# Window attention beside a mixture of experts: two key halves in one product, and the softmax passage one step later

## The chip, the cores and the metric

The kernel runs on one core of one Trainium2 chip. The metric is device microseconds of one execution. The kernel before takes 686.98 us, the median of 3 runs (686.58 to 687.01). All times are in us unless ns is said.

## The reference

```python
xn = layernorm(x)                                    # x: 32 sequences of 256 tokens, 128 channels
# attention branch
h = relu(xn @ nm_w1 + nm_b1);  m = h @ nm_w2 + nm_b2
q, k, v = m @ q_w + q_b, m @ k_w + k_b, m @ v_w + v_b
scores = (q . k in a window of 32 tokens to either side) / sqrt(128)
a = softmax(scores) @ v (over the window)
# expert branch: 16 experts, the 8 best per token, and a shared one
s = sigmoid(xn @ gate_w.T);  chosen = top8(s + expert_bias);  c = 2.826 * s / sum(s of chosen)
y = sum over experts e of c[e] * (silu(xn @ w_gate[e].T) * (xn @ w_up[e].T)) @ w_down[e].T
y = y + the same with the shared weights, without c
out = x + a + y
```

All of it is float32. Every big operand is split into a high part that the product engine takes as it is and a low rest, and a product of two such operands is three products: high by high, high by low, low by high.

## The kernel before, in words

The 8192 tokens go through in 16 groups of 512 (two sequences of 256, each in two tiles of 128 queries). A group has 17 steps: step 0 is the shared expert, steps 1 to 16 the routed ones. Each engine has a program written by hand (`slot(g, par, s)`), walked through group by group and step by step; the attention and the routing of the same and of the next group are hung into its steps (`when(g, s, fresh)` gives the step, with another one for group 0; `more` and `last` leave out what the last group doesn't need). Nothing else orders the work: every engine runs its list in order and waits on semaphores.

For step k of a group I write:

- gate(k) and up(k): three products of 512 columns each on PE into `ps_g` and `ps_u` (two banks each, used in turn), lines 466 and 476. gate(k) waits until silu(k-2) is done, up(k) until h_lo(k-2) is done.
- silu(k): ACT, line 717, from `ps_g`. silu_c(k): POOL, line 1262, times the routing weight.
- h(k): DVE, line 1134, silu_c times `ps_u` in place. h_hi(k): ACT, line 725, the high part. h_lo(k): DVE, line 1140, the rest.
- down(k): three products of 512 on PE into `ps_y`, line 486.

In its step s PE issues gate(s+1), down(s-3) and up(s), ACT h_hi(s-1) and silu(s+1), DVE h(s-1) and h_lo(s-1), POOL silu_c(s+1). Between these stand, for the group's attention:

- PE: `scores(seq)`, line 430, one bank per sequence, both tiles of queries in it, three products of 160 columns for each tile (step 3 for sequence 0, step 5 for sequence 1); `turn_probs(seq)`, line 437, three transposes of 128 columns (end of step 7, and step 9); `attend`, line 447, products of 256 and 160 columns (steps 13 and 14); `value_proj`, line 456, in step 0 of the next group; `hid_proj` of the next group, three products of 512, at the end of step 7 behind the transposes; the gate product of the router (`gate`, line 419) in step 4.
- POOL: `mask_terms(seq)`, line 1246: the window mask plus a term for each key, two operations for each sequence.
- DVE: `row_max(seq)`, line 1025: score plus mask and the row's maximum in one operation for each tile; `normalise_probs`, lines 1033 and 1037; `gate_sum` (step 5), lines 866 and 870, four transposes and a sum of the router's product; `route_scores` (step 7), lines 877 to 881; then the choice of 8 and the weights in steps 8 to 11, for the next group.
- ACT: `gate_exp` (router, line 674) and `prob_exp(0)` (line 706) in step 5, `prob_exp(1)` in step 6 behind h_hi(5), the two table loads around them (silu and the exponential are in different tables), `prob_hi` in steps 7 and 9.

So ACT's list between silu(6) and silu(7) is: table load, the router's exponential, two exponentials, h_hi(5), two exponentials, table load. I call this the passage.

## Time and profile before

| what | value |
|---|---|
| median of 3 runs | 686.98 us |
| profiled execution | 687.21 us, span 685.4 us |
| PE busy | 676.9 us, 99% of the span |
| PE weight loads | 553.8 us, 81% |
| DVE busy | 597.6 us, 87% |
| ACT busy | 437.2 us, 64% |
| POOL busy | 443.0 us, 65% |
| granted clock of PE | 9 or more tenths in all 40 slices |
| chain that ended last | PE 90%, DVE 4%, DMA 3%, ACT 1%, issue 1% |

The chain is followed back from the last instruction: at each step to what released it, or to the instruction before it on its engine. Busy time of PE says little by itself, because matmuls are pipelined and their ends are modelled; the starts of successive products in the timeline say how long each really takes.

### The profile page before, as it was taken

How to read it: one execution, taken by the hardware profiler on the slowest of the kernel's cores; microseconds unless marked ns; L12 is line 12 of the kernel's file. 1: busy time of each engine (PE TensorE's matmuls, PEld its weight loads, DVE VectorE, ACT ScalarE, POOL GpSimd, SP SyncE). 2: the span in 40 equal slices, each digit the busy share in tenths (PEclk: the TensorE clock that was granted, in tenths of full speed). 3: DMA queues.
4: the chain of work that ended last, by engine and by line, in shares of the span. 5: the costliest groups of instructions: out<-in, count | busy, mean ns of one | idle time of the engine just before them, and what ended most of it. 6: DMA issues, size and time to landing. Idle time of an engine off the chain costs nothing.

```text
span 685.4 us, 10455 instructions
## 1 busy us (share of the span) xinstructions
PE 676.9 (99%) x3172; PEld 553.8 (81%) x3172; DVE 597.6 (87%) x1640; ACT 437.2 (64%) x874; POOL 443.0 (65%) x400
## 2 busy tenths in 40 slices
PE   7999999999999999999999999999999999999997
PEld 6877788888888888888888888888888888888885
DVE  7998989888889898889888898898889888898775
ACT  5775656657675575666657665575756757666573
POOL 4785666666667756766666667766667567666553
PEclk9999999999999999999999999999999999999999
DMA  8607255252623617155261633617145161631500
GB/s 266 236 9 272 61 186 185 93 232 73 233 113 124 235 46 277 62 173 198 65 260 51 252 116 104 254 45 278 63 163 208 49 262 47 220 121 63 231 0 16
DMA packets 38040, 101.80 MB, mean 149 GB/s; under 512 B 8672, under 2 KB 18144, under 8 KB 29920
## 3 DMA queue, kind: packets, MB, share of 16 engines
q1 hardware_dynamic: 37984, 101.14, 41.1%
q8 instruction: 25, 0.41, 0.2%
q14 instruction: 31, 0.25, 0.1%
HBM read 92.42 MB, written 8.70 MB: 148 GB/s over the span
## 4 chain that ended last, share of the span: by engine, by line
PE 90%; DVE 4%; DMA 3%; ACT 1%; issue 1%; SPq 1%; POOL 0%; DVEq 0%; ACTq 0%
PE ps_y L486 26%; PE ps_u L476 26%; PE ps_g L466 25%; PE bank L408 3%; PE bank L447 3%; PE bank L430 3%; PE bank L437 1%; PE ps_y L456 1%; DMA exp_raw<-wexp 1%; DMA h_dram<-exp_raw 1%; DVE ps_u L1134 1%; PE bank L419 1%; DVE h_lo L1140 1%; DMA exp_raw<-h_dram 0%; DVE prob_n L1037 0%
## 5 line engine op out<-in xcount | busy, mean ns | idle before, releaser
L1262 POOL TENSOR_TENSOR silu_c<-silu,comb_b 128x512 f32<-128x512 f32 x252 | 325.3, 1294 | 220.5 <-ACT silu L717 219.6
L725 ACT ACTIVATE h_hi<-ps_u 128x512 fp32r<-128x512 f32 x272 | 162.9, 599 | 232.9 <-DVE ps_u L1134 232.8
L1140 DVE TENSOR_TENSOR h_lo<-ps_u,h_hi 128x512 fp32r<-128x512 f32 x272 | 186.0, 684 | 37.3 <-ACT h_hi L725 30.4
L1134 DVE TENSOR_TENSOR ps_u<-silu_c,ps_u 128x512 f32<-128x512 f32 x256 | 177.1, 692 | 28.5 <-PE ps_u L476 24.2
L717 ACT ACTIVATE silu<-ps_g 128x512 f32<-128x512 f32 x272 | 162.0, 596 | 0.2
L476 PE MATMUL ps_u<-xn_hi,exp_w_hi 128*128 128x512 f32 x272 | 111.2, 409 | 0.7 <-DVE h_lo L1140 0.6
L486 PE MATMUL ps_y<-h_hi,exp_w_hi 128*128 128x512 f32 x272 | 109.4, 402 | 0.9 <-DVE h_lo L1140 0.4
L466 PE MATMUL ps_g<-xn_hi,exp_w_hi 128*128 128x512 f32 x272 | 108.1, 397 | 1.3 <-ACT silu L717 1.3
L486 PE MATMUL ps_y<-h_lo,exp_w_hi 128*128 128x512 f32 x272 | 107.7, 396 | 0.0
L476 PE MATMUL ps_u<-xn_hi,exp_w_lo 128*128 128x512 f32 x272 | 107.6, 396 | 0.0
L486 PE MATMUL ps_y<-h_hi,exp_w_lo 128*128 128x512 f32 x272 | 107.3, 394 | 0.0
L466 PE MATMUL ps_g<-xn_hi,exp_w_lo 128*128 128x512 f32 x272 | 106.9, 393 | 0.0
L476 PE MATMUL ps_u<-xn_lo,exp_w_hi 128*128 128x512 f32 x272 | 106.7, 392 | 0.0
L466 PE MATMUL ps_g<-xn_lo,exp_w_hi 128*128 128x512 f32 x272 | 105.8, 389 | 0.0
L476 PEld LDWEIGHTS ps_u<-xn_hi,exp_w_hi 128*128 128x128 f32 x272 | 51.2, 188 | 14.0 <-DVE h_lo L1140 3.2
L466 PEld LDWEIGHTS ps_g<-xn_hi,exp_w_hi 128*128 128x128 f32 x272 | 51.0, 188 | 13.9 <-issue 2.0
L486 PEld LDWEIGHTS ps_y<-h_hi,exp_w_lo 128*128 128x128 f32 x272 | 51.3, 189 | 12.2
L476 PEld LDWEIGHTS ps_u<-xn_hi,exp_w_lo 128*128 128x128 f32 x272 | 51.2, 188 | 12.2
L466 PEld LDWEIGHTS ps_g<-xn_lo,exp_w_hi 128*128 128x128 f32 x272 | 51.3, 188 | 12.1
L466 PEld LDWEIGHTS ps_g<-xn_hi,exp_w_lo 128*128 128x128 f32 x272 | 51.0, 188 | 12.3
L486 PEld LDWEIGHTS ps_y<-h_hi,exp_w_hi 128*128 128x128 f32 x272 | 51.2, 188 | 11.2 <-DVE h_lo L1140 0.8
L486 PEld LDWEIGHTS ps_y<-h_lo,exp_w_hi 128*128 128x128 f32 x272 | 51.3, 189 | 9.9
(156 smaller groups left out, 989.2 us busy)
## 6 DMA issues: line engine op xcount, KB each, us to landing
comb_b<-c_dram SPq DMA_DIRECT2D x63, 1024.0 KB, 7.2
mom_b<-st_dram SPq DMA_DIRECT2D x13, 512.0 KB, 3.7
xres<-x_t SPq DMA_DIRECT2D x16, 256.0 KB, 2.6
out_t<-xres SPq DMA_DIRECT2D x16, 256.0 KB, 2.0
xin<-x SPq DMA_DIRECT2D x15, 256.0 KB, 3.2
h_dram<-exp_raw SPq DMA_DIRECT2D x60, 64.0 KB
exp_raw<-h_dram SPq DMA_DIRECT2D x15, 256.0 KB, 3.1
xn<-x_t SPq DMA_DIRECT2D x13, 256.0 KB, 3.3
```

Of the source, the lines that this page charges most:

```text
L408: done = mm(dst[:], att_w[a][:, w, :], parts[b][:], start=n == 0, stop=n == 2)
L419: done = mm(bank[0][:], gate_w[:].rearrange("p q c -> p (q c)"), xn_t[par][n][:], start=n == 0, stop=n == 1)
L430: done = mm(dst[:, t * SEQ:t * SEQ + WIN], q_t[a][:, q0:q0 + P], hid_t[b][:, k0:k0 + WIN], start=n == 0, stop=n == 2)
L447: done = mm(bank[2][:, col:col + wide], hid_n[a][:, seq * 2 + kb, :], p_t[b][:, seq, kb, 0:wide], start=kb == 0 and n == 0, stop=kb == 1 a ...
L466: done = mm(ps_g[i][:], exp_w[a][:, s, 0:P], xn_t[par][b][:], start=n == 0, stop=n == 2)
L476: done = mm(ps_u[i][:], exp_w[a][:, s, P:2 * P], xn_t[par][b][:], start=n == 0, stop=n == 2)
L486: done = mm(ps_y[:], exp_w[a][:, s, 2 * P:3 * P], h_t[i][b][:], start=s == 0 and n == 0, stop=s == STEPS - 1 and n == 2, skip_group_check= ...
L717: A(silu[i][:], ps_g[i][:], ACT.Silu).then_inc(s_silu, 1)
L725: A(h_t[hbuf(par, s)][0][:], ps_u[(par + s) % 2][:], ACT.Copy).then_inc(s_h_hi, 1)
L1134: V.tensor_tensor(ps_u[i][:], src[:], ps_u[i][:], ALU.mult).then_inc(s_h, 1)
L1140: V.tensor_tensor(t[1][:], ps_u[(par + s) % 2][:], t[0][:].bitcast(F32), ALU.subtract)\
L1262: G.tensor_tensor(silu_c[i][:], silu[i][:], comb_b[:, s1 - 1, :], ALU.mult).then_inc(s_silu_c, 1)
```

## The change

All of it applies from group 2 on (`wide(g)`), groups 0 and 1 stay as they were except for the places of some steps.

- High and low part of the keys (`hid_t`) now lie in one tensor `hid_hl`. For each tile of queries, one product of 320 columns takes the high part of the queries against both halves of the keys, and one of 160 the low part of the queries against the high half, added to the front half of the result. Each tile of queries has its own bank (`window_bank`), so both sequences use the same two banks one after the other.
- The rear half (queries by low keys) is read by ACT (`low_scores`), which adds the key's term and writes `low_k`; POOL adds the mask in one operation for each sequence; `row_max` adds the front half and writes its result to `prob` in SBUF, where the exponentials and the normalising now read and write.
- `scores(0)` moves from step 3 to 2, `scores(1)` stays in 5 and now waits for the row maximum of sequence 0. `mask_terms(1)` moves on POOL from step 3 to 5. `row_max(1)` moves from 6 to 7, the exponentials from 5 and 6 to 6 and 7 (the router's with them), `normalise_probs(0)` from 6 to 7, `turn_probs` from 7 and 9 to 8 and 10 (the first now also waits for the second row maximum), `prob_hi` from 7 and 9 to 8 and 10, `prob_lo(1)` from 10 to 11. `hid_proj` stays at the end of step 7.
- `route_scores` stays in step 7 of DVE but goes from ahead of h_lo(6) to behind it.

```diff
-            def scores(seq):
+            def scores(g, seq):
+                if wide(g):
+                    for t in range(2):
+                        q0 = seq * SEQ + t * P
+                        k = slice(seq * SEQ + t * (P - HALF), seq * SEQ + t * (P - HALF) + WIN)
+                        dst = window_bank[t]
+                        mm(dst[:, 0:2 * WIN].rearrange("p (h c) -> p h c", h=2), q_t[0][:, q0:q0 + P],
+                           hid_hl[:, :, k], start=True, stop=False, skip_group_check=True)
+                        done = mm(dst[:, 0:WIN], q_t[1][:, q0:q0 + P], hid_hl[:, 0, k], start=False, stop=True,
+                                  skip_group_check=True)
+                    done.then_inc(S[f"sc{seq}"], 1)
+                    return
...
-                if s == when(g, 3, 5):
+                if s == when(g, 2 if wide(g) else 3, 5):
...
                 if s == when(g, 5, 7):
-                    scores(1)
+                    if wide(g):
+
+                        pe.wait_ge(S["nmax0"], g + 1)
+                    scores(g, 1)
...
-                if s == when(g, 9, 12):
+                if s == when(g, 10, 12):
                     pe.wait_ge(S["pn1"], g + 1)
                     turn_probs(1)
...
-                if s == when(g, 7, 10):
+                if s == when(g, 7, 10) and not last(g):
+                    hid_proj(g + 1, 1 - par)
+                if s == when(g, 8, 10):
                     pe.wait_ge(S["pn0"], g + 1)
+                    if wide(g):
+
+                        pe.wait_ge(S["nmax1"], g + 1)
                     turn_probs(0)
-                    if not last(g):
-                        hid_proj(g + 1, 1 - par)
...
+            def low_scores(g, seq):
+
+                act.wait_ge(S[f"sc{seq}"], g + 1)
+                act.wait_ge(S["key_term"], 2 * g + seq + 1)
+                for t in range(2):
+                    n = 2 * seq + t
+                    done = A(low_k[:, n, :], window_bank[t][:, WIN:2 * WIN], ACT.Identity, bias=key_term[:, n:n + 1])
+                done.then_inc(S[f"low{seq}"], 1)
...
-                if s == when(g, 5, 8):
+                if wide(g) and s == 2:
+                    low_scores(g, 0)
+                if wide(g) and s == 5:
+                    low_scores(g, 1)
+                if s == when(g, 6, 8):
                     if more:
                         gate_exp(g + 1)
                     prob_exp(g, 0)
...
-                if s == when(g, 6, 9):
+                if s == when(g, 7, 9):
                     prob_exp(g, 1)
...
-                if s == when(g, 6, 9):
+                if s == when(g, 7, 9):
                     normalise_probs(g, 0)
-                if s == 7 and more and not first(g):
-                    route_scores(g + 1)
...
-                if s == when(g, 6, 9):
+                if s == when(g, 7, 9):
                     row_max(g, 1)
...
-                if first(g) and s == 9:
-                    route_scores(1)
+                if s == when(g, 7, 9) and not last(g):
+                    route_scores(g + 1)
...
+                if wide(g):
+                    n = slice(2 * seq, 2 * seq + 2)
+                    pool.wait_ge(S[f"low{seq}"], g + 1 - (TURNED - 1))
+                    G.tensor_tensor(mask_k[:, n, :], mask[:], low_k[:, n, :], ALU.add).then_inc(S["mask_k"], 1)
+                    return
```

How the instructions now follow one another, at three places. On PE, the second block of scores of a group (step 5), with the gate products ahead of it and the down products behind; `q_hi`, `q_lo` are the queries, `hid_hi`, `hid_lo`, `hid_hl` the keys. Before:

```order
L466 MATMUL ps_g<-xn_hi,exp_w_lo 128x512
L430 MATMUL bank<-hid_hi,q_hi 128x160
L430 MATMUL bank<-hid_lo,q_hi 128x160
L430 MATMUL bank<-hid_hi,q_lo 128x160
L430 MATMUL bank<-hid_hi,q_hi 128x160
L430 MATMUL bank<-hid_lo,q_hi 128x160
L430 MATMUL bank<-hid_hi,q_lo 128x160
L486 MATMUL ps_y<-h_hi,exp_w_hi 128x512
```

Now:

```order
L492 MATMUL ps_g<-xn_hi,exp_w_lo 128x512
L445 MATMUL bank<-hid_hl,q_hi 128x320
L447 MATMUL bank<-hid_hl,q_lo 128x160
L445 MATMUL bank<-hid_hl,q_hi 128x320
L447 MATMUL bank<-hid_hl,q_lo 128x160
L512 MATMUL ps_y<-h_hi,exp_w_hi 128x512
```

Six products of 160 columns have become two of 320 and two of 160, each with its own weight load.

On ACT, the passage with its exponentials, from h_hi(4) on, in a group from 2 on; `bank` and `prob` are the scores, `low_k` the new rear half. Before:

```order
L725 ACTIVATE h_hi<-ps_u 128x512
L717 ACTIVATE silu<-ps_g 128x512
L674 ACT_TABLE_LOAD
L674 ACTIVATE gate_e<-gate_s 128x64
L706 ACTIVATE bank,row_sum<-bank,neg_max 128x160 x2
L725 ACTIVATE h_hi<-ps_u 128x512
L706 ACTIVATE bank,row_sum<-bank,neg_max 128x160 x2
L717 ACT_TABLE_LOAD
L717 ACTIVATE silu<-ps_g 128x512
```

Now:

```order
L768 ACTIVATE h_hi<-ps_u 128x512
L760 ACTIVATE silu<-ps_g 128x512
L742 ACTIVATE low_k<-bank,key_term 128x160 x2
L768 ACTIVATE h_hi<-ps_u 128x512
L760 ACTIVATE silu<-ps_g 128x512
L709 ACT_TABLE_LOAD
L709 ACTIVATE gate_e<-gate_s 128x64
L749 ACTIVATE prob,row_sum<-prob,neg_max 128x160 x2
L768 ACTIVATE h_hi<-ps_u 128x512
L749 ACTIVATE prob,row_sum<-prob,neg_max 128x160 x2
L760 ACT_TABLE_LOAD
L760 ACTIVATE silu<-ps_g 128x512
```

The passage began behind silu(6) and ended with silu(7); it now begins behind silu(7) and ends with silu(8), and two copies of scores stand where it was.

On DVE, from the router's sum in step 5 on; `ps_u` is h(k), the lines with ISA are the row maximum. Before:

```order
L870 TENSOR_REDUCE gate_s<-gate_h 128x64
L1140 TENSOR_TENSOR h_lo<-ps_u,h_hi 128x512
L1025 ISA bank,neg_max<-bank,mask_k 128x160
L1025 ISA neg_max 128x1
L1025 ISA bank,neg_max<-bank,mask_k 128x160
L1025 ISA neg_max 128x1
L1134 TENSOR_TENSOR ps_u<-silu_c,ps_u 128x512
L1033 RECIPROCAL row_inv<-row_sum 128x2
L1037 TENSOR_SCALAR prob_n<-bank,row_inv 128x160 x2
L1140 TENSOR_TENSOR h_lo<-ps_u,h_hi 128x512
L1134 TENSOR_TENSOR ps_u<-silu_c,ps_u 128x512
L877 TENSOR_SCALAR gate<-gate_e 128x64
```

Now:

```order
L1184 TENSOR_TENSOR h_lo<-ps_u,h_hi 128x512
L1071 ISA prob,neg_max<-bank,mask_k 128x160
L1071 ISA neg_max 128x1
L1071 ISA prob,neg_max<-bank,mask_k 128x160
L1071 ISA neg_max 128x1
L1178 TENSOR_TENSOR ps_u<-silu_c,ps_u 128x512
L1079 RECIPROCAL row_inv<-row_sum 128x2
L1083 TENSOR_SCALAR prob_n<-prob,row_inv 128x160 x2
L1184 TENSOR_TENSOR h_lo<-ps_u,h_hi 128x512
L924 TENSOR_SCALAR gate<-gate_e 128x64
L926 RECIPROCAL score<-gate 128x64
L928 TENSOR_TENSOR select<-score,ebias 128x64
```

Ahead of the second piece stand, now, the sum, h_lo(4) and h(5) alone: its first row is h_lo(5), and the row maximum of sequence 1 follows that instead of h_lo(4). The normalising goes with it, and the routing's scores have come behind h_lo(6).

## Rows read from the trace of the kernel before

**Rows 1.** Timeline of PE: start, duration, engine, line, operation; last value product, groups 7 and 8.
```profile
310.32 0.39 PE L456 MATMUL ps_y<-z_hi,att_w_lo 128*128 128x512 f32 x1
...
351.66 0.39 PE L456 MATMUL ps_y<-z_hi,att_w_lo 128*128 128x512 f32 x1
```

**Rows 2.** Timeline of PE: first block of scores in group 7, and products behind it.
```profile
316.11 0.24 PE L430 MATMUL bank<-hid_hi,q_hi 128*128 128x160 f32 x1
316.19 0.27 PE L430 MATMUL bank<-hid_lo,q_hi 128*128 128x160 f32 x1
...
317.02 0.39 PE L486 MATMUL ps_y<-h_lo,exp_w_hi 128*128 128x512 f32 x1
317.25 0.40 PE L486 MATMUL ps_y<-h_hi,exp_w_lo 128*128 128x512 f32 x1
```

**Rows 3.** Timeline of PE: the product of 256 columns in attend, group 7.
```profile
340.81 0.28 PE L447 MATMUL bank<-p_hi,hid_n_hi 128*128 128x256 f32 x1
340.93 0.23 PE L447 MATMUL bank<-p_lo,hid_n_hi 128*128 128x160 f32 x1
```

**Rows 4.** Timeline of PE: first products of gate(9) and gate(10), group 7.
```profile
328.68 0.40 PE L466 MATMUL ps_g<-xn_hi,exp_w_hi 128*128 128x512 f32 x1
...
330.76 0.40 PE L466 MATMUL ps_g<-xn_hi,exp_w_hi 128*128 128x512 f32 x1
```

**Rows 5.** Timeline of ACT: h_hi(4), silu(6), end of the first two exponentials, silu(7).
```profile
321.65 0.60 ACT L725 ACTIVATE h_hi<-ps_u 128x512 fp32r<-128x512 f32 x1 [1.38 <-DVE ps_u L1134]
322.15 0.59 ACT L717 ACTIVATE silu<-ps_g 128x512 f32<-128x512 f32 x1
...
324.86 0.20 ACT L706 ACTIVATION_READ_ACCUMULATOR bank<-bank,neg_max 128x1 f32 x1
...
327.73 0.60 ACT L717 ACTIVATE silu<-ps_g 128x512 f32<-128x512 f32 x1
```

**Rows 6.** Timeline of DVE: h(4), h_lo(4), h(5), h_lo(5), h(6), routing, h(7), h_lo(7).
```profile
320.92 0.70 DVE L1134 TENSOR_TENSOR ps_u<-silu_c,ps_u 128x512 f32<-128x512 f32 x1 [0.41 <-PE ps_u L476]
...
323.17 0.69 DVE L1140 TENSOR_TENSOR h_lo<-ps_u,h_hi 128x512 fp32r<-128x512 f32 x1
...
324.30 0.73 DVE L1134 TENSOR_TENSOR ps_u<-silu_c,ps_u 128x512 f32<-128x512 f32 x1
...
325.88 0.68 DVE L1140 TENSOR_TENSOR h_lo<-ps_u,h_hi 128x512 fp32r<-128x512 f32 x1
326.48 0.69 DVE L1134 TENSOR_TENSOR ps_u<-silu_c,ps_u 128x512 f32<-128x512 f32 x1
327.08 0.19 DVE L877 TENSOR_SCALAR gate<-gate_e 128x64 f32<-128x64 f32 x1
...
327.89 0.23 DVE L881 TENSOR_TENSOR select<-score,ebias 128x64 f32<-128x64 f32 x1
...
329.81 0.70 DVE L1134 TENSOR_TENSOR ps_u<-silu_c,ps_u 128x512 f32<-128x512 f32 x1 [0.27 <-POOL silu_c L1262]
...
331.51 0.68 DVE L1140 TENSOR_TENSOR h_lo<-ps_u,h_hi 128x512 fp32r<-128x512 f32 x1
```

**Rows 7.** Timeline of ACT and PE, last group: silu(7), second product of gate(9).
```profile
657.78 0.60 ACT L717 ACTIVATE silu<-ps_g 128x512 f32<-128x512 f32 x1
...
658.76 0.40 PE L466 MATMUL ps_g<-xn_lo,exp_w_hi 128*128 128x512 f32 x1
```

**Rows 8.** Groups by line and shape, whole span: count, busy us and mean ns.
```profile
L706 ACT ACTIVATE bank<-bank,neg_max 128x160 f32<-128x160 f32 x64 | 23.1, 360 | 0.0
...
L685 ACT ACTIVATE q_hi<-bank,vecs 128x512 fp32r<-128x512 f32 x16 | 11.2, 703 | 0.0
...
L670 ACT ACTIVATE xn_hi<-xn 128x512 fp32r<-128x512 f32 x13 | 8.3, 637 | 0.0
...
L670 ACT ACTIVATE xn_hi<-bank 128x512 fp32r<-128x512 f32 x3 | 1.8, 600 | 0.9 <-PE bank L558 0.9
```

**Rows 9.** The same view: POOL's product of silu and weight.
```profile
L1262 POOL TENSOR_TENSOR silu_c<-silu,comb_b 128x512 f32<-128x512 f32 x252 | 325.3, 1294 | 220.5 <-ACT silu L717 219.6
```

More of the change, by code:

```diff
@@ L118, in layer @@
         hid = sb("hid", [P, T])
-        hid_t = [sb("hid_hi", [P, T], F32R), sb("hid_lo", [P, T], F32R)]
+        hid_hl = sb("hid_hl", [P, 2, T], F32R)
+        hid_t = [hid_hl[:, half, :] for half in range(2)]
         q_t = [sb("q_hi", [P, T], F32R), sb("q_lo", [P, T], F32R)]
@@ L168, in layer @@
         score_bank = [bank[2], bank[1]]
+        window_bank = [bank[2], bank[1]]
         s_watt_in = sem("watt_loaded")
@@ L245, in when, with wide @@
             return fresh if first(g) else s
+        def wide(g):
+            return g + 1 >= TURNED
         def last(g, ahead=0):
@@ L596, in att_early @@
                     pe.wait_ge(S["q_lo"], g + 1)
-                    scores(0)
+                    if g + 1 == TURNED:
+                        pe.wait_ge(S["xn_lo"], TURNED)
+                    scores(g, 0)
                 if s == when(g, 4, 7) and more:
@@ L1023, in row_max @@
                     n = 2 * seq + t
-                    win = score_bank[seq][:, t * SEQ:t * SEQ + WIN]
+                    src = window_bank[t][:, 0:WIN] if wide(g) else score_bank[seq][:, t * SEQ:t * SEQ + WIN]
                     done = V.tensor_tensor_reduce(
-                        out=win, in0=win, in1=mask_k[:, n, :],
+                        out=scored(g, seq, t), in0=src, in1=mask_k[:, n, :],
                         scale=-1.0, scalar=-TAKEN, op0=ALU.add, op1=ALU.min, accum_out=neg_max[:, n:n + 1])
@@ L1076, in att @@
                     route_match(g + 1)
-                if s == when(g, 10, 13):
+                if s == when(g, 11, 13):
                     prob_lo(g, 1)
@@ L1276, in slot @@
                     mask_terms(g, 0)
-                if s == when(g, 3, 6):
+                if s == when(g, 5 if wide(g) else 3, 6):
                     mask_terms(g, 1)
```

17 lines of the change are left out of this document (11 added, 6 removed).

## The prediction, made before the changed kernel ran

> **What bounds the kernel now.** I read the table above first: PE is busy for nearly the whole span and its clock is at the higher level throughout, so the product stream is the suspect. The timeline of PE then decides. The last value product of one group stands at 310.32, that of the next at 351.66 [rows 1], so a group takes 41.34 us, and inside it one product of 512 columns starts every 0.23 us with no hole; 317.02 to 317.25 is one such step [rows 2]. So in such a group nothing but PE's own work sets the time, and any saved product is worth its full length, as long as nobody else becomes late. The reader should therefore look second at who is nearly late. ACT has to pass two exponentials and two table loads between two silus, and the last group, which has one PE job less there (no hid_proj for a next group), shows what happens when the room is gone: the silu starts at 657.78, ends 0.60 later at 658.38, and the gate products wait for it. Their second product starts at 658.76, so the first effectively at 658.53 [rows 7]: a wait on this silu restarts PE 0.15 us after the silu's end.
>
> I write gate(k), silu(k), h(k) (product on DVE), h_hi(k), h_lo(k), up(k) for step k of group 7; all times are those of the trace of before, 310 to 352 us.
>
> **What the change saves on PE.** Six products of 160 columns run from 316.11 to 317.02 together with one product of 512 [rows 2]: 0.91 - 0.23 = 0.68 us for the six, 0.113 each, though the first, whose successor's weights were already there, took only 0.08 (316.11 to 316.19). So the short ones pay for their weight loads, not for their columns. The new block is two products of 320 and two of 160. No row has 320 columns: 256 take 0.12 (340.81 to 340.93) [rows 3], 512 take 0.23; between them by columns, 0.15. The new block is 2 x (0.15 + 0.113) = 0.53 and saves 0.15. Bounds: if 320 cost as much as 512, 2 x (0.23 + 0.113) = 0.69 and nothing is saved; if the loads hid wholly, 2 x (0.15 + 0.08) = 0.46 and 0.22 is saved. I take 0.15, being much nearer to 256 columns than to 512. Two blocks in 14 groups: 28 x 0.15 = 4.2 us, if PE stays the bound. Merely moving a job (scores 0 from step 3 to 2, the two sets of transposes, the place of hid_proj) costs PE nothing.
>
> **What the change moves, and what becomes late.** On ACT, the whole passage (table load, gate exponential, two exponentials, h_hi, two exponentials, table load) goes from between silu(6) and silu(7) to between silu(7) and silu(8). Before, silu(6) starts at 322.15 and silu(7) at 327.73 [rows 5]: 5.58 us, in which ACT never waits long. silu(7) ends at 328.33 and is needed by gate(9) at 328.68 [rows 4]; with the 0.15 of the restart the room is 0.2 us. That is all there was.
>
> Now the same passage one step later, by rows. PE is 0.15 early after the first block, so h(4), which waits for up(4), starts at 320.92 - 0.15 = 320.77 [rows 6]. On DVE the gate sums come behind it: h(4) to h_lo(4) is 320.92 to 323.17, 2.25, so h_lo(4) starts at 323.02 and h(5), 0.60 behind (as 325.88 + 0.60 = 326.48, where the next h follows), at 323.62. The row maximum, which used to stand between them (it is why h(5) was at 324.30), is gone from here. h to h_hi is 0.73 (320.92 to 321.65), h_hi to silu 0.50 [rows 5, 6]: h_hi(5) at 324.35, silu(7) at 324.85. Add the passage, 5.58: silu(8) starts at 330.43, ends at 331.03, and PE restarts at 331.18. gate(10), which needs silu(8), stood at 330.76 [rows 4] and would be at 330.46 after both savings. **PE waits 0.72 us**, so gate(10) is 0.42 later than it is now. The reason is plain in the rows: from gate(6) to gate(9) PE had a score block to do, from gate(7) to gate(10) it has none, 0.68 less time for the same passage.
>
> A second wait follows. The first two exponentials end at 324.86 + 0.20 = 325.06, 2.91 behind the start of their silu, so now at 327.76; from there to h_lo of that step DVE takes 0.82 (325.88) [rows 5, 6], so h_lo(6) starts at 328.58, and 0.60 later come the routing's scores, which the change puts behind h_lo: 327.08 to the last one's end, 327.89 + 0.23, about 1.0. h(7) then starts at 330.18, h_lo(7) 1.70 later (329.81 to 331.51) at 331.88; it ends at 332.57, and up(9), which needs it, restarts at 332.72. PE would be there at 331.18 + 6 x 0.23 = 332.57. That is 0.15 more. Sum without any price for new operands: 0.42 + 0.15 = 0.57 us later per group.
>
> The exponentials now read and write SBUF instead of PSUM. The one pair of rows for the source is 637 ns from SBUF against 600 from PSUM [rows 8]; the destination has no such pair, and as the exponential overlaps with what follows it, nothing at all is the lower end. I take 0.04 each; as upper end twice that and a little, 0.09. Two of them lie ahead of h_lo(6), so up(9) moves by 0.08, to 0.65 per group (upper end 0.17, to 0.75); all four lie ahead of silu(8), which reaches up(9) no later than that.
>
> The Trainium skill, in "ScalarE: Activation LUTs", section "Step-by-step: what each stage is for", says that ScalarE writes PSUM faster than SBUF, which speaks against this move; no run here shows it. By the 0.833 ns a column of its section "What ACT_TABLE_LOAD costs", q_hi's 703 ns [rows 8] would be 410 at 160 columns, an estimate, 0.05 above the exponential's 360: then up(9) moves by another 0.10, and the time below would be 1.3 us longer.
>
> **What stays hidden.** The four new ACT copies (low scores) lie at steps 2 and 5, where ACT has free time before its next h_hi: from 322.5, two of them at no more than 0.45 each, against h_hi(5) at 324.35. POOL's one sum instead of two for the mask takes at most the 1.29 of a 512-wide one [rows 9]: silu(6) ends at 322.6, silu_c(6) at 323.9, the mask at 325.2, and the row maximum, behind h_lo(5), comes at 325.6. If that cover were gone, it would delay h(6) and not ACT, which is then in its passage until 327.76. PE's new wait for the first row maximum is free too: on DVE it stands ahead of h_lo(3) and h(4), so it is over before 320.2, and the second block comes at about 321.3. What is queued behind that wait is all of PE, so if it were late, every 0.1 us would cost 1.4 us in all. The routing's scores end 1.0 us later against PE, but the weights they lead to are for the next group. The moved issues on SP: none.
>
> **The sum.** Groups 2 to 14 have the passage, the gate exponential and the new scores: 13 x 0.65 = 8.5 us. The last has no gate work and waited already; I take +0.3 for it, between -0.3 and +0.9. Together +8.8: 687.21 of the profiled execution becomes 696.0. That execution lies 0.23 above the median of 686.98, so **695.8 us**. Ends: with the larger saving (0.22, which also brings h(4) forward by 0.07), no price for SBUF and no second wait, 0.35 per group and -0.3, +4.2, 691.2; with nothing saved (0.15 later) and the dearer exponentials, 0.90 per group and +0.9, +12.6, 699.6. About 0.2% (1.4 us) is what a measurement of this kernel can tell from no change.
>
> **Rivals.**
> 1. Faster: PE stays the bound and the 4.2 us come out, 682.8 us. For it: PE's stream has no hole now, and three engines have idle time. Against it: the room of 0.2 us before gate(9) and the last group's wait. It decides from the point where silu(8) ends by 330.31, 0.72 earlier than I work out; that needs silu(7) to start as soon as its products are there rather than behind h(5) and the gate sums, which ACT's order does not allow. 10%.
> 2. The change doesn't do what it says: the product of 320 in two pieces of a bank is read no faster than 512 columns, nothing is saved, and the passage still moves. h(4) is then back at 320.92, so each group is 0.15 worse, with the dear exponentials 0.90: 699.6 us. For it: no row shows a product with its moving operand in two pieces. Against: 256 columns took half the time of 512. 8%.
> 3. The two waits half cancel: PE, stopped at gate(10), gives DVE the time to catch up, so that only some 0.1 per group is left over the saving, or DVE finishes the gate sums sooner. 13 x 0.1 = +1.3, 688.3. Against: h_lo(7) hangs on the exponentials, not on PE. 4%.
>
> **How the numbers follow.** My case, 691.2 to 699.6, has 78%. Slower takes it and rival 2: 86%; no difference within 0.2% is rival 3, 4%; faster is rival 1, 10%. The range 690.5 to 700 leaves out rivals 1 and 3 and a little on either side.
>
> **What would show it.** In the profile after: score blocks with steps of about 0.15 and 0.11; idle time of PE in every group from 2 on, in the wait list under the silu of step 8 (gate line, about 0.7 a group) and under h_lo (up line); a group period near 42.0 instead of 41.34; PE below 99%. A period of 41.04 with no idle PE would prove rival 1. If PE waits elsewhere (at the second score block on the first row maximum, at the transposes), my chain of steps is wrong even if the total fits.

## The result: 12 us slower, and the profile after

The changed kernel takes 699.0 us, the median of 4 runs (698.25 to 700.13), against 687.0 for the kernel before on the same chip. The ratio is 1.0176, with a 95% interval of 1.0157 to 1.0194: slower, as forecast, and 3.2 us above the forecast of 695.8. The profiled execution is the 700.13 one, with a span of 698.2. It came to its first value product 2 us later than the kernel before (61.83 against 59.82 us from the start): between 10 and 16 us the granted clock was 0.50, the lower of its two levels, where before shows 1.00; PE had been busy for 5.2 of the 6 us ahead of that. The spans of the other three executions are 696.2, 696.4 and 697.7. Nothing below rests on that stretch.

I call the time from one group's last value product to the next one's the period. The timeline of PE of the changed kernel (start, duration, engine, line, operation) answers to [rows 1]:

```profile
316.60 0.39 PE L482 MATMUL ps_y<-z_hi,att_w_lo 128*128 128x512 f32 x1
...
358.69 0.39 PE L482 MATMUL ps_y<-z_hi,att_w_lo 128*128 128x512 f32 x1
```

So this period is 42.09 instead of 41.34. All 13 groups from 2 to 14 have about the same: 42.10 in the middle, 41.35 before. Group 1 went from 43.77 to 44.25, the last from 37.93 to 38.55. 13 x 0.75 + 0.48 + 0.62 = 10.9 us, and 685.4 + 10.9 = 696.3, which is the span of the two shortest executions. That of 697.7 left no trace, so its extra 1.4 us have no cause here.

The page of the changed kernel, busy time and the chain that ended last (by engine):

```profile
PE 683.2 (98%) x3116; PEld 549.9 (79%) x3116; DVE 599.7 (86%) x1640; ACT 455.7 (65%) x930; POOL 424.2 (61%) x372
...
PE 62%; DVE 15%; ACT 15%; issue 4%; DMA 2%; POOL 1%; SPq 0%; DVEq 0%; ACTq 0%
```

The busy share of PE fell by one point only, but the chain says what happened: it was PE for 90%, and is now PE for 62%, with DVE and ACT at 15% each. It leaves PE for DVE and ACT and comes back, again and again. The list of waits (engine, line, releaser: us in total, times, longest) names the places where it comes back:

```profile
PEld ps_g L492 <- ACT silu L760: 11.4, 15, 0.8
PEld ps_u L502 <- DVE h_lo L1184: 8.2, 23, 0.9
...
PEld ps_y L512 <- DVE xres L1061: 4.7, 15, 0.5
```

Weight loads run ahead of products, so these totals are not what PE loses. What it loses is read from the starts of products. First the score block, PE's timeline, answering to [rows 2]:

```profile
320.30 0.31 PE L445 MATMUL bank<-hid_hl,q_hi 128*128 128x320 f32 x1
320.45 0.24 PE L447 MATMUL bank<-hid_hl,q_lo 128*128 128x160 f32 x1
320.52 0.35 PE L445 MATMUL bank<-hid_hl,q_hi 128*128 128x320 f32 x1
320.71 0.24 PE L447 MATMUL bank<-hid_hl,q_lo 128*128 128x160 f32 x1
320.78 0.43 PE L512 MATMUL ps_y<-h_hi,exp_w_hi 128*128 128x512 f32 x1
321.05 0.39 PE L512 MATMUL ps_y<-h_lo,exp_w_hi 128*128 128x512 f32 x1
```

320.30 to 321.05, less one product of 512, is 0.75 - 0.23 = 0.52. It was 0.68: the block saves 0.16.

Then the wait for silu(8), answering to [rows 4]:

```profile
336.49 0.49 PE L463 MATMUL bank<-ident,prob_n 128*128 128x128 f32 x3
337.51 0.50 PE L492 MATMUL ps_g<-xn_hi,exp_w_hi 128*128 128x512 f32 x1 [0.53 <-ACT silu L760]
337.84 0.40 PE L492 MATMUL ps_g<-xn_lo,exp_w_hi 128*128 128x512 f32 x1
```

The second product starts at 337.84, so gate(10) effectively at 337.61; three transposes from 336.49 at 0.11 each end by 336.82. PE stands for 0.8 us. On ACT, answering to [rows 5]:

```profile
330.76 0.60 ACT L768 ACTIVATE h_hi<-ps_u 128x512 fp32r<-128x512 f32 x1 [1.19 <-DVE ps_u L1178]
331.25 0.59 ACT L760 ACTIVATE silu<-ps_g 128x512 f32<-128x512 f32 x1
331.87 1.28 ACT L709 ACT_TABLE_LOAD   x1
...
336.86 0.60 ACT L760 ACTIVATE silu<-ps_g 128x512 f32<-128x512 f32 x1
```

silu(7) stands at 331.25 and silu(8) at 336.86, 5.61 apart. silu(8) ends at 337.46, and PE restarts 0.15 later, as in [rows 7]. On DVE h(4), h_lo(4), h(5), h_lo(6) and h_lo(7), answering to [rows 6]:

```profile
327.20 0.69 DVE L1178 TENSOR_TENSOR ps_u<-silu_c,ps_u 128x512 f32<-128x512 f32 x1
...
329.43 0.69 DVE L1184 TENSOR_TENSOR h_lo<-ps_u,h_hi 128x512 fp32r<-128x512 f32 x1
330.04 0.68 DVE L1178 TENSOR_TENSOR ps_u<-silu_c,ps_u 128x512 f32<-128x512 f32 x1
...
334.90 0.69 DVE L1184 TENSOR_TENSOR h_lo<-ps_u,h_hi 128x512 fp32r<-128x512 f32 x1
...
338.00 0.67 DVE L1184 TENSOR_TENSOR h_lo<-ps_u,h_hi 128x512 fp32r<-128x512 f32 x1
```

h(4) has no bracket here. Before it had idled 0.41 for up(4) [rows 6]; now DVE comes to it without a pause, which matters below. From h(4) to gate(10) are 337.61 - 327.20 = 10.41 us.

Two smaller waits show in the timeline of PE's weight loads, at down(0) and at up(12):

```profile
322.93 0.19 PEld L512 LDWEIGHTS ps_y<-h_hi,exp_w_hi 128*128 128x128 f32 x1 [0.30 <-DVE xres L1061]
...
345.66 0.19 PEld L502 LDWEIGHTS ps_u<-xn_hi,exp_w_hi 128*128 128x128 f32 x1 [0.31 <-DVE h_lo L1184]
```

The neighbouring products start at 322.66, 322.93 and 323.27 in step 3 and at 345.39, 345.67 and 346.00 in step 12: each pair of steps takes 0.61 where two products take 0.46, so 0.15 is lost at each. These three places account for the loss: 0.79 + 0.15 + 0.15, less twice the 0.16 saved, is 0.77 a group, and the period grew by 0.75.

Last the groups by line and shape (count, busy us and mean ns), answering to [rows 8]:

```profile
L749 ACT ACTIVATE prob<-prob,neg_max 128x160 f32<-128x160 f32 x56 | 23.2, 415 | 0.0
...
L742 ACT ACTIVATE low_k<-bank,key_term 128x160 f32<-128x160 f32 x56 | 19.1, 402 | 0.0
...
L906 DVE TENSOR_TENSOR xn_lo<-xn,xn_hi 128x512 fp32r<-128x512 f32 x13 | 17.5, 1347 | 0.0
...
L749 ACT ACTIVATE bank<-bank,neg_max 128x160 f32<-128x160 f32 x8 | 2.9, 362 | 0.0
```

An exponential in SBUF takes 415 ns, one in PSUM 362 in the same execution. The third line I had not expected: `xn_lo`, untouched by the change, took 0.69 us before.

### The profile page after: what moved, and what is told of

Same layout as the page of the kernel before. It is cut to its first block, busy times and chain, and to the rows that moved or that the text cites. A ratio compares the mean times of both kernels' runs of the same rounds, so it can differ in the third digit from the quotient of the medians.

```text
span 698.2 us, 10413 instructions
## 1 busy us (share of the span) xinstructions
PE 683.2 (98%) x3116; PEld 549.9 (79%) x3116; DVE 599.7 (86%) x1640; ACT 455.7 (65%) x930; POOL 424.2 (61%) x372
## 4 chain that ended last, share of the span: by engine, by line
PE 62%; DVE 15%; ACT 15%; issue 4%; DMA 2%; POOL 1%; SPq 0%; DVEq 0%; ACTq 0%
PE ps_g L492 18%; PE ps_u L502 18%; PE ps_y L512 18%; DVE ps_u L1178 6%; ACT h_hi L768 4%; ACT prob L749 3%; DVE h_lo L1184 3%; ACT L760 3%; ACT L709 3%; PE bank L473 3%; ACT silu L760 2%; DVE gate_h L913 2%; PE bank L423 2%; PE ps_y L482 1%; DMA h_dram<-exp_raw 1%
## 5 line engine op out<-in xcount | busy, mean ns | idle before, releaser
L492 PE MATMUL ps_g<-xn_hi,exp_w_hi 128*128 128x512 f32 x272 | 109.7, 403 | 7.9 <-ACT silu L760 7.9
L502 PE MATMUL ps_u<-xn_hi,exp_w_hi 128*128 128x512 f32 x272 | 112.7, 414 | 0.9 <-DVE h_lo L1184 0.8
```

The source lines that it names most:

```text
L492: done = mm(ps_g[i][:], exp_w[a][:, s, 0:P], xn_t[par][b][:], start=n == 0, stop=n == 2)
L502: done = mm(ps_u[i][:], exp_w[a][:, s, P:2 * P], xn_t[par][b][:], start=n == 0, stop=n == 2)
```

## The experiments

My theory after the first look: the saving on PE is real, and PE loses more to waits than it saves. The waits end two chains of ACT and DVE that run close together, one through the passage to silu(8), one through h_lo(6), the routing's scores and h(7) to h_lo(7), with two small waits beside them. The rivals: one single wait, so that whatever removes it brings the gain out; or a price of the new work itself.

**1. The passage without its table loads.**

```diff
-                A(silu[i][:], ps_g[i][:], ACT.Silu).then_inc(s_silu, 1)
+                A(silu[i][:], ps_g[i][:], ACT.Tanh).then_inc(s_silu, 1)
```

The experts' function is tanh here; in this run's trace no table load stands between it and the exponentials.

> The changed kernel with tanh in place of silu (the function of the experts is changed), so that ACT needs no table switch: the passage is 2 x 1.29 us shorter, everything else stays. Theory (PE waits for silu(8) because the passage now ends there): the wait of 0.80 us a group at gate(10) goes, the period falls from 42.10 to 41.15 to 41.30 us, the time to 684 to 687 us. Rival (the new work itself costs: four ACT copies, POOL sums, operands in SBUF, DVE): the period stays above 41.8, the time above 695 us.

Measured: 696.23 us, ratio 1.0141 (1.0124 to 1.0158), period 41.77. The wait at gate(10) is gone, yet only 2.8 of the 12 us or more that I expected came. (By the period it is 13 x 0.33 = 4.3 us; this execution, too, comes to its first value product 2 us late, at 61.97, and why is not shown.) The timelines of this run: PE at up(9); DVE's h_lo(6), the last of the routing's scores, h(7) and h_lo(7); POOL beside them.

```profile
337.59 0.50 PE L502 MATMUL ps_u<-xn_hi,exp_w_hi 128*128 128x512 f32 x1 [0.39 <-DVE h_lo L1184]
```

```profile
332.68 0.69 DVE L1184 TENSOR_TENSOR h_lo<-ps_u,h_hi 128x512 fp32r<-128x512 f32 x1
...
334.09 1.31 DVE L928 TENSOR_TENSOR select<-score,ebias 128x64 f32<-128x64 f32 x1
335.33 0.68 DVE L1178 TENSOR_TENSOR ps_u<-silu_c,ps_u 128x512 f32<-128x512 f32 x1
...
336.86 0.67 DVE L1184 TENSOR_TENSOR h_lo<-ps_u,h_hi 128x512 fp32r<-128x512 f32 x1
```

```profile
334.03 1.30 POOL L1311 TENSOR_TENSOR silu_c<-silu,comb_b 128x512 f32<-128x512 f32 x1 [1.95 <-ACT silu L760]
```

A second wait stands right behind the first: up(9) waits for h_lo(7), because the last of the routing's scores took 1.31 us beside POOL's product, for an operation that took 0.23 before [rows 6]. My expectation had counted one wait only. But this wait is of the run's own making: silu(8) is earlier, so POOL's product behind it now falls beside the routing's scores, and that costs 1.08, more than the 0.67 that PE loses at up(9) by the starts of products. In the changed kernel the same operation takes 0.23, so this run doesn't show that h_lo(7) is late there; runs 2 and 4 are better witnesses.

**2. The moves without the new products.**

```diff
         def wide(g):
-            return g + 1 >= TURNED
+            return False
```

> The changed kernel with the wide form switched off in every group: products of 160 columns, scores in PSUM and mask as before, scores(0) in step 3, and only the moves of steps left (exponentials in 6 and 7, transposes in 8 and 10, routing's scores behind h_lo(6)). Theory: the moves make the wait, with 0.45 to 0.57 us a group more than before from silu(8) and some 0.15 from the later h_lo, period 41.8 to 42.1, time 693 to 697 us, as group 1, which has the moves alone, lost 0.48. Rival (new work and operands cost): as before, 41.35 and 687 us.

Measured: 697.06, ratio 1.0148 (1.0133 to 1.0163), period 42.01. The moved steps alone cost 0.66 a group of the 0.75, although here the exponentials are in PSUM, no copies exist and the mask takes two operations as before. So most of the loss is in the order, and the new products and their helpers together come to +0.09 a group in this order. The timelines of ACT, silu(7) and silu(8), and of PE's weight loads, at up(9):

```profile
328.94 0.59 ACT L760 ACTIVATE silu<-ps_g 128x512 f32<-128x512 f32 x1
...
334.40 0.60 ACT L760 ACTIVATE silu<-ps_g 128x512 f32<-128x512 f32 x1
```

```profile
336.64 0.19 PEld L502 LDWEIGHTS ps_u<-xn_hi,exp_w_hi 128*128 128x128 f32 x1 [0.37 <-DVE h_lo L1184]
```

The passage is 5.46 long here, not 5.61, and gate(10) stands 20.88 behind the value product. It has the operations of the passage before, which took 5.58. The timeline of ACT in the kernel before, h_hi(5):

```profile
325.06 0.60 ACT L725 ACTIVATE h_hi<-ps_u 128x512 fp32r<-128x512 f32 x1
```

It starts 0.03 behind the end of h(5) [rows 6] and 0.20 behind the start of the last row of the two exponentials [rows 5]; in run 2 it is 0.09 between the same two rows. So the old passage holds a wait of ACT for h(5), and that is nearly all of the 0.12. In the new order PE waits a second time at up(9), for h_lo(7), and loses 0.22 there by the starts of products (336.31 and 336.99 around it, 0.68 for two products).

**3. The router's sum one DVE step later.**

```diff
-                if s == when(g, 5, 8) and more:
+                if s == when(g, 6, 8) and more:
                     gate_sum(g + 1)
```

> The changed kernel with DVE's gate sums one step later, behind h(5) instead of ahead of h_lo(4). Theory: silu(7) hangs on h(5), which then starts as soon as up(5) is there, 0.28 us earlier; the wait at gate(10) falls from 0.80 to about 0.52, period 41.8, time 694 to 695.5 us. Rival (silu(7) hangs on its own products, or the wait at gate(10) is not set by the start of the passage): no change, 698 us.

Measured: 693.73, ratio 1.0100 (1.0085 to 1.0115), period 41.83, 0.27 less. h(5) no longer stands behind the sum, so the passage starts earlier and the step from the last transpose to gate(10) shrinks from 0.80 to 0.52. As expected: h(5) and with it the passage did hang on the sum. The time is a little below the expected range because group 1 gains too (43.15 instead of 44.25).

**4. Other work for PE ahead of gate(10).**

```diff
+                early = not first(g) and s == 9
+                if early:
+                    down(*before(g, par, s, LAG))
...
-                if not first(g) or s >= LAG:
+                if not early and (not first(g) or s >= LAG):
```

> The changed kernel with PE's step 9 in another order: down(6) ahead of gate(10). Theory with one wait only: the 0.69 us of down(6) cover most of the 0.80, period 41.4, time 688 to 689.5 us. Theory with two chains close behind one another (silu(8), and h_lo(7), which up(9) needs and which ends at 338.67 in the trace, PE there at 338.30): only 0.2 is won, the rest appears as a wait of up(9) for h_lo(7), period 41.9, time 695 to 696 us.

Measured: 697.93, ratio 1.0163 (1.0148 to 1.0178), period 42.10. Nothing was won, where one wait would have given 41.4 and two close together 41.9. The timeline of PE's weight loads has the first ones of gate(10), up(9) and up(10):

```profile
335.83 0.19 PEld L492 LDWEIGHTS ps_g<-xn_hi,exp_w_hi 128*128 128x128 f32 x1 [0.30 <-ACT silu L763]
...
337.04 0.19 PEld L502 LDWEIGHTS ps_u<-xn_hi,exp_w_hi 128*128 128x128 f32 x1 [0.69 <-DVE h_lo L1187]
...
339.66 0.19 PEld L502 LDWEIGHTS ps_u<-xn_hi,exp_w_hi 128*128 128x128 f32 x1 [0.17 <-DVE h_lo L1187]
```

0.69 of products now covers most of the wait for silu(8), and PE stands at up(9) for h_lo(7) instead. By the starts of products it loses 0.13 at gate(10), 0.52 at up(9) and 0.18 at up(10), there for h_lo(8). So three chains end close together, not two: up(9) comes 0.17 earlier than in the changed kernel (22.25 against 22.42 behind the value product), and the wait for h_lo(8) gives that back (up(10) at 24.87 against 24.85). No operation of DVE on the way to h_lo(7) is longer here than in the changed kernel, so this decides against the single wait.

**5. up(3) ahead of down(0) in step 3,** to cover the wait for `xres`.

```diff
+                late = wide(g) and s == 3
+                if late:
+                    up_proj(g, par, s)
...
-                up_proj(g, par, s)
+                if not late:
+                    up_proj(g, par, s)
```

> In step 3 of the groups with the new scores, up(3) goes ahead of down(0); nothing else changes against the changed kernel. Theory (four separate waits add up: gate(10) on silu(8), up(9) on h_lo(7) close behind, up(12) on h_lo(10), and down(0) in step 3 on the addition that empties its bank, 0.145 a group): the last of them disappears because 0.69 of other products stand before it, and as the next wait is not before gate(10), the group becomes shorter only by what does not come back there. Rival A: ACT's passage hangs on h(4) and up(4), so 0.145 less on PE before it brings the whole chain 0.145 forward: period 41.96 in place of 42.10, 697.0. Rival B: the chain hangs on something that PE doesn't set, the wait at gate(10) grows by 0.145 and the period stays 42.1, 699.

Measured: 697.93, ratio 1.0156 (1.0140 to 1.0173), period 42.11. The wait for `xres` went, the period didn't move: rival B. The cause is on DVE. Its h(4) stands 10.62 behind the value product (324.92 against 314.30), as in the changed kernel (327.20 - 316.60 = 10.60), though up(4)'s last product now starts at 324.30. Whatever made DVE late lies before h(4), and the one operation there that had become longer is `xn_lo`. In the changed kernel, DVE and POOL in their timelines:

```profile
323.38 1.34 DVE L906 TENSOR_TENSOR xn_lo<-xn,xn_hi 128x512 fp32r<-128x512 f32 x1
```

```profile
323.30 0.88 POOL L1290 TENSOR_TENSOR mask_k<-mask,low_k 128x320 f32<-128x320 f32 x1
```

and in the kernel before, beside POOL's sums of one tensor and a column (DVE, then POOL):

```profile
317.11 0.69 DVE L859 TENSOR_TENSOR xn_lo<-xn,xn_hi 128x512 fp32r<-128x512 f32 x1
```

```profile
317.05 1.88 POOL L1246 TENSOR_SCALAR mask_k<-mask,key_term 128x160 f32<-128x160 f32 x2
...
320.18 1.34 POOL L1246 TENSOR_SCALAR mask_k<-mask,key_term 128x160 f32<-128x160 f32 x2
```

**6. and 7. POOL's mask sum with one tensor as input,** with run 5's edit and without it. Both leave the window mask out of the scores.

```diff
-                    G.tensor_tensor(mask_k[:, n, :], mask[:], low_k[:, n, :], ALU.add).then_inc(S["mask_k"], 1)
+                    for t in range(2):
+                        n = 2 * seq + t
+                        done = G.tensor_scalar(mask_k[:, n, :], low_k[:, n, :], key_term[:, n:n + 1], None, ALU.add)
+                    done.then_inc(S["mask_k"], 1)
```

> up(3) ahead of down(0) in step 3, as in that run, and POOL's sum for the mask replaced by two operations of 160 columns with one tensor as input (the key's term added to the copied rear half once more; the window mask itself is left out of the scores). Theory (POOL's sum of two tensors and DVE's xn_lo, which also reads two tensors from SBUF, hinder each other: xn_lo takes 1.34 in the changed kernel where it took 0.69, and this alone made h(4) late on DVE, so that PE's 0.145 in step 3 won nothing): xn_lo is back at about 0.7, h(4) waits for up(4) on PE again, 0.145 earlier against the value product, and the period falls from 42.1 to about 41.96, 696 us. Rival (xn_lo is slow for another reason, or h(4) is late because of something else): xn_lo stays above 1.2, or the period stays at 42.1, 698 us.

> The changed kernel with POOL's sum for the mask replaced by two operations with one tensor as input (the window mask is left out of the scores); up(3) stays behind down(0). Theory (PE's 0.145 in step 3 and DVE's long xn_lo lie side by side ahead of h(4), and both must go before anything is won): xn_lo at about 0.7, but the period stays at 42.05 to 42.1, 698 to 699 us. Rival (DVE alone sets h(4)): the period falls by 0.1 to 0.15 with this edit alone, to 41.95 to 42.0.

Measured: with run 5's edit 695.62, ratio 1.0124 (1.0109 to 1.0139), period 41.93; without it 697.78, ratio 1.0161 (1.0143 to 1.0179), period 42.07. The timeline of DVE with both edits, `xn_lo` and h(4):

```profile
320.14 0.68 DVE L910 TENSOR_TENSOR xn_lo<-xn,xn_hi 128x512 fp32r<-128x512 f32 x1
...
323.76 0.70 DVE L1182 TENSOR_TENSOR ps_u<-silu_c,ps_u 128x512 f32<-128x512 f32 x1 [0.22 <-PE ps_u L502]
```

`xn_lo` is short again, h(4) waits for PE again, and stands 10.41 behind the value product (313.35). The four periods, 42.10 with neither edit, 42.11 and 42.07 with one, 41.93 with both, show that the wait on PE and the long operation on DVE lie side by side ahead of h(4): either alone hides the other.

**8. The new products in the old steps:** exponentials in steps 5 and 6 again, row maximum and normalising of sequence 1 in 6, transposes in 7 and 9, routing's scores ahead of h_lo(6).

```diff
-                if s == when(g, 6, 8):
+                if s == when(g, 5, 8):
                     if more:
                         gate_exp(g + 1)
                     prob_exp(g, 0)
...
-                if s == when(g, 7, 9):
+                if s == when(g, 6, 9):
                     prob_exp(g, 1)
```

> The new products of scores, the copies by ACT and the single mask sum stay, but the passage stands in the step where it stood before the change: exponentials in steps 5 and 6, row maximum and normalising of sequence 1 in 6, transposes in 7 and 9, routing's scores ahead of h_lo(6). Theory (the saving on PE is real, and the step decides; but the second copy on ACT, POOL's sum and the row maximum of sequence 1 now stand in a row ahead of the second exponentials, which the old step has no room for): PE waits longer than in the changed kernel, at gate(9), by 1.0 to 1.6 a group; period 42.2 to 42.8, 700 to 708. Rival (only the move of the passage costs, the new work itself fits anywhere): the period is 41.0 to 41.3, 682 to 687.

Measured: 704.87, ratio 1.0258 (1.0243 to 1.0274), period 42.58. The size is as expected, the place is not: by the starts of products PE loses 1.05 at up(7), for h_lo(5), and only 0.27 at gate(9), where I had expected all of it. The timelines of PE, at up(7), and of DVE, at the row maximum:

```profile
333.98 0.50 PE L502 MATMUL ps_u<-xn_hi,exp_w_hi 128*128 128x512 f32 x1 [0.77 <-DVE h_lo L1186]
```

```profile
331.38 0.33 DVE L1071 CUSTOM_DVE_ANT_0 prob<-bank,mask_k 128x160 f32<-128x160 f32 x1 [1.22 <-POOL mask_k L1292]
```

DVE stands for 1.22 at the row maximum of sequence 1, waiting for POOL's sum, which has its turn behind POOL's product for step 6; h(5) is queued behind that, and h_lo(5) hangs on h(5). With the new products the old steps are worse than the moved ones, so the move was not needless: it needed more than was given.

**9. Five moves at once:** runs 3, 4 and 5 together, `turn_probs(1)` back in step 9, and `prob_lo(1)` from step 11 to 12.

```diff
-                if s == when(g, 10, 12):
+                if s == when(g, 9, 12):
                     pe.wait_ge(S["pn1"], g + 1)
                     turn_probs(1)
...
-                if s == when(g, 11, 13):
+                if s == when(g, 12, 13):
                     prob_lo(g, 1)
```

> Five moves at once, with the new products of scores kept: the router's sum on DVE one step later (behind h(5)), down(6) ahead of gate(10), the transposes of sequence 1 back to step 9, up(3) ahead of down(0) in step 3, the low part of the probabilities of sequence 1 one step later on DVE. Theory (the loss is only waits of PE behind two chains that run close together, ACT's passage to silu(8) and DVE's to h_lo(7), and two small ones): with the two chains each relieved, most of the 0.32 saved on the score blocks comes out: period 41.0 to 41.3, 682 to 687. Rival (the new work itself costs PE or ACT something that no order can hide, such as the slower exponentials): the period stays above 41.6, over 691.

Measured: 689.22 (8 runs), ratio 1.0030 (1.0019 to 1.0040), period 41.53, between the theory's 41.3 and the rival's 41.6. One wait is left, shown by the timeline of PE; that of DVE, from h(8) to h_lo(8), shows why:

```profile
334.23 0.50 PE L502 MATMUL ps_u<-xn_hi,exp_w_hi 128*128 128x512 f32 x1 [0.25 <-DVE h_lo L1191]
```

```profile
331.91 0.70 DVE L1185 TENSOR_TENSOR ps_u<-silu_c,ps_u 128x512 f32<-128x512 f32 x1 [0.35 <-POOL silu_c L1318]
332.51 0.48 DVE L1096 TENSOR_TENSOR p_lo<-bank,p_hi 128x320 fp32r<-128x320 f32 x1
...
333.48 0.69 DVE L1191 TENSOR_TENSOR h_lo<-ps_u,h_hi 128x512 fp32r<-128x512 f32 x1
```

It is up(10), one step later than I looked: h(8) waits for POOL's product, which waits for silu(8), and the low part of the probabilities and the matching of the best eight stand ahead of h_lo(8).

**10. In addition the routing's scores behind h_lo(7).**

```diff
-                if s == when(g, 7, 9) and not last(g):
+                if s == when(g, 8, 9) and not last(g):
                     route_scores(g + 1)
...
-                if s == when(g, 8, 10) and more:
-                    route_max(g + 1)
...
+                if s == when(g, 9, 10) and more:
+                    route_max(g + 1)
```

> As the run with five moves, and in addition the routing's scores go behind h_lo(7) on DVE, with the choice of eight one step later. Theory (h_lo(7) is late because the routing's scores, 1 us and more beside POOL's product, stand between h_lo(6) and h(7)): if the run with five moves still has a wait of up(9) for h_lo(7), it goes here, and the period is 41.0 to 41.1, 682 to 684. Rival: the routing's scores are not what makes h_lo(7) late, and the period is that of the run with five moves within 0.05; or the weights of the next group now come late, and the wait shows at its first steps.

Measured: 704.65, ratio 1.0254 (1.0239 to 1.0269), period 42.60. A clear miss: my expectation took the wait left in run 9 to be for h_lo(7), and the edit put more work ahead of h_lo(8), the operation that PE had really been waiting for. h_lo(8) came 2.0 us behind h(8) (341.08 against 339.07) where run 9 has 1.57, and h(8) itself stood behind the scores.

**11. Run 9 with the passage begun earlier:** in step 5, too, up goes ahead of down, so that h(5), and silu(7) behind it, come earlier; and the low parts of the probabilities go to steps 12 and 13.

```diff
-                late = wide(g) and s == 3
+                late = wide(g) and s in (3, 5)
...
-                if s == when(g, 9, 12):
+                if s == 12:
                     prob_lo(g, 0)
...
-                if s == when(g, 12, 13):
+                if s == 13:
                     prob_lo(g, 1)
```

> The run with five moves and two more: in step 5 of the groups with the new scores, up(5) goes ahead of down(2), so that silu(7), where the passage begins, no longer waits for h(5) (in the run with five moves silu(7) stood at 324.14 in group 7, its products done near 323.6); and the low parts of the probabilities go to steps 12 and 13 of DVE, so that they no longer stand ahead of h_lo(8). Theory (the one wait left in the run with five moves, 0.5 a group at up(10), hangs on silu(8), POOL's product of 1.3, h(8) and h_lo(8), and so on the start of the passage): the passage starts about 0.5 earlier, the wait goes, and the whole saving of 0.32 on the score blocks comes out: period 41.0 to 41.15, 681.5 to 684.5. Rival (the end of this chain hangs on DVE's own order, the matching of the best eight ahead of h_lo(8), or another wait stands right behind): the period is 41.3 to 41.5, 686 to 689.

Measured: **682.86 us**, ratio 0.9940 (0.9927 to 0.9952), period 41.07: faster than both kernels. The chain of its page by engine, and silu(7) and silu(8) in its timeline of ACT:

```profile
PE 92%; DVE 4%; DMA 2%; ACT 1%; issue 1%; SPq 0%; DVEq 0%; ACTq 0%
```

```profile
322.08 0.59 ACT L767 ACTIVATE silu<-ps_g 128x512 f32<-128x512 f32 x1
...
327.68 0.60 ACT L767 ACTIVATE silu<-ps_g 128x512 f32<-128x512 f32 x1
```

The value product of this group is at 308.31, so the passage starts 13.77 behind it, not 14.65 (331.25 - 316.60) as in the changed kernel. The same passage, 5.60 long, now fits, and PE is the bound again. silu(7) still stands behind h_hi(5), which waits 0.31 for h(5); my expectation that it would no longer wait for h(5) was wrong, but h(5) itself is earlier. The trace parts the two edits: against run 9, h(8) comes 0.46 earlier behind the value product (21.55 for 22.01), with the passage, and h_lo(8) 0.67 earlier (22.91 for 23.58), the other 0.21 being the low part that no longer stands ahead of it. No run has one of the two alone.

**12. The order of run 11 with the old products,** mask sums and exponentials (scores of sequence 0 in step 3, up first in step 5 only).

```diff
         def wide(g):
-            return g + 1 >= TURNED
+            return False
...
-                late = wide(g) and s in (3, 5)
+                late = g + 1 >= TURNED and s == 5
```

> The same order of work, but with the six old products of 160 columns in place of the two of 320 and two of 160, the mask's two sums on POOL, and the exponentials in PSUM (scores of sequence 0 in step 3, as they were before the change). Theory (in an order without waits the new products are worth their 0.16 a block): PE bound at the period of the kernel before, 41.35 to 41.5, 687 to 690, so that the same order with the new products is 0.30 to 0.35 a group faster. Rival (the new products are worth nothing, the order is all): the two have the same period within 0.05.

Measured: 686.61 (11 runs), ratio 0.9994 (0.9985 to 1.0003), period 41.37. The order alone is worth nothing; the new products in it are worth 0.30 a group, 3.75 us in all. In run 2's order they were worth less than nothing.

## Why the prediction was right, and where its steps were not

- **The saving: right.** 0.16 a block against 0.15. The steps were 0.15 and 0.07 for the first pair, 0.19 and 0.07 for the second, and 0.27 for the product behind: not the 0.15 and 0.11 of the forecast one by one, but the same in the sum.
- **From h(4) to gate(10): right as a chain, and to the hundredth by luck.** Worked out: from h(4) at 320.77 to PE's restart at 331.18, 10.41. Measured: 10.41. The wait arose as described, 0.80 against 0.72, and h(4) to silu(7) took 4.05 for 4.08. But the passage of 5.58 was taken over from before as it was, and two errors cancel in it. Run 2 shows both: ACT did wait in the old passage, 0.12, for h(5), and the four exponentials in SBUF make the new one 0.15 longer than the 5.46 that it takes without that wait.
- **"PE is 0.15 early after the first block, so h(4) starts at 320.77": wrong.** h(4) stands 10.60 behind the value product, exactly where it was. The sentence that merely moving a job "costs PE nothing" fails here. Two things took the 0.15, each of them enough: down(0), no longer behind the score block, waits for the bank that `xres` empties, and `xn_lo` takes 0.66 longer beside POOL's new sum. I had asked of that sum only when it ends, not what it does to DVE meanwhile. Runs 5, 6 and 7 show both. gate(10) was therefore 0.57 later (21.01 against 20.44 behind the value product), not 0.42.
- **"A second wait follows" at up(9): not there in this kernel,** though close. Normalising from SBUF takes 301 ns for a tile instead of 380, and there are two tiles of it ahead of h_lo(6) and two more ahead of h_lo(7): h_lo(6) came 0.66 behind the end of the exponentials at 334.24, not 0.82, and h_lo(7) 1.54 behind h(7), not 1.70. So h_lo(7) ended in time, at 338.67 for an up(9) that starts at 339.01. Run 2, where the normalising reads PSUM, has the wait: 0.22, for the 0.15 worked out without the dearer exponentials; run 4 shows that in the changed kernel, too, h_lo(7) lies directly behind the first wait. What came in its place is 0.15 at up(12), a wait I had not foreseen: h_lo(10) was late on DVE, with `prob_lo(1)` moved into that step. That move alone is not the cause, for run 2 has it too and no such wait, with h_lo(10) 0.21 earlier (28.15 against 28.36 behind the value product). No run undid the move alone; in runs 9 and 11, which move it on, no such wait is left. The cause stays open in part.
- **The exponentials' price: about right, and it did reach ACT's path.** 53 ns each (415 against 362), my guess was 40; the estimate of 410 from q_hi was nearer. The Trainium skill, "ScalarE: Activation LUTs", section "Step-by-step: what each stage is for", says that writing PSUM is the faster of the two; the measurement agrees, though here source and destination changed together. For the four in a passage I had 0.16; against run 2, which has the same order of steps and the exponentials in PSUM, it is 0.15 (5.61 against 5.46), and gate(10) is 0.13 later (21.01 against 20.88) with h(4) 10.60 behind the value product in both. That the passage is only 0.03 longer than before is the old wait for h(5), not a hidden price.
- **Group 1: left out.** It has no new products but all the moves, and lost 0.48. The last group lost 0.62, of which I had taken 0.3. These two and 0.75 for my 0.65 in 13 groups are the 2.1 us between 8.8 and 10.9.
- **Rival 1,** the PE-bound 682.8 us, was wrong for this order of work and is what the right order gives: 682.86 in run 11. (That it fits so closely is partly luck: each group with the new products gains 0.28 for the 0.30, and group 1, which has none, gains 0.52.) Its condition, silu(8) 0.72 earlier, "which ACT's order does not allow", was true of ACT's list and not of PE's: up(5) ahead of down(2), with the router's sum behind h(5), gives it. The condition is silu(8) at 330.31 - 0.60 - 310.32 = 19.39 behind the value product; it stands at 19.37 in run 11, 20.26 in the changed kernel. Rival 2 falls by the measured block, rival 3 by the waits.

## What to carry to other kernels

A saved product on a full engine is worth its length only in an order in which nobody else gets late: here the same products, with their helpers, were worth +1.23 us a group in the old steps (run 8 against the kernel before), +0.09 in the moved ones (the changed kernel against run 2) and -0.30 in the last order (run 11 against run 12); plus is slower. When a wait is removed and nothing is won, look for a second chain that ends just behind it or beside it, and test pairs of edits, not only single ones. For each operation added to an engine with idle time, ask what runs on the other engines in the same microsecond, and not only when it ends.

## What the runs showed of the hardware that I had not expected

In these traces DVE and POOL hinder each other where DVE reads two tensors from SBUF. `xn_lo` (two inputs in SBUF) took 1347 ns in the mean of 13 beside POOL's sum of two tensors, and 684 in runs 6 and 7, where that sum reads one tensor. There POOL is the one that pays: in the kernel before its pair of operations beside `xn_lo`, at 317.05, took 1.88 us and the next pair, at 320.18, took 1.34; in run 6 the pair beside `xn_lo` took 1.88 again, and the mean of all 56 operations is 810 ns, beside 686 for the same form in the first two groups of the changed kernel. h_lo, with one of its inputs in PSUM, kept its 683 ns throughout. The most was lost by a short operation: the routing's 64-column sum went from 0.23 to 1.31 us beside silu_c in run 1. The Trainium skill, "SBUF — State Buffer", section "SBUF: two separate sides", describes what the two share as a pair of ports under an exclusive lock, held for a whole instruction; the 1.31 us beside an instruction of 1.30 agree with that. The same section gives the lock to whoever starts first; in run 6 POOL's pair of operations starts at 320.08 and `xn_lo` at 320.14 isn't held up. That would fit if a POOL operation with one tensor is treated otherwise, or if DVE was really the first, since starts on POOL are rough in a trace; this stays open. In run 11 `xn_lo` is still 1351 ns long, and PE is the bound all the same: what the collision costs depends on the order, too.
